# Long convolution: squares of keys on ACT, wrapped terms on POOL, key products formed one head ahead

## The chip, the cores and the metric

The kernel runs on one core of a Trainium2 chip. The metric is the device time of one execution in microseconds. Before the change three runs took 3490.82 to 3492.23 us, with a median of 3491.84 us. Five engines share a core: TensorE (PE), VectorE (DVE), ScalarE (ACT), GpSimd (POOL) and SyncE (SP), which issues the loads. Each has its own stream of instructions, and they meet only through semaphores.

## What is computed

The kernel is a decoder of two layers. The change touches one of its six mixing steps, the long convolution, which is given here in full; the others stand as names.

```python
# B, S, D = 8, 256, 512; ctx is a second input of the same shape as x; everything is fp32
def _L0_xattn_ref(k, v, q, ssm_kernel, D, head_dim):      # called with k = v = ctx, q = x, head_dim = 8
    B, HD, L = k.shape                                     # 8, 256, 512
    H = HD // head_dim                                     # 32 heads of 8 rows
    k_, v_, q_ = (t.reshape(B, H, head_dim, L) for t in (k, v, q))
    kv = jnp.einsum('bhil,bhjl->bijhl', k_, v_)            # product of row i and row j, element by element
    y = irfft(rfft(kv, 2 * L) * rfft(ssm_kernel, 2 * L))[..., :L]   # causal convolution along L with head h's filter
    out = y + kv * D[None, None, None, :, None]
    out = jnp.einsum('bijhl,bhil->bjhl', out, q_)          # times row i of x, summed over i
    return jnp.transpose(out, (0, 2, 1, 3)).reshape(B, H * head_dim, L)

x = _layernorm(x + attention(x))
x = _layernorm(x + _L0_xattn_ref(ctx, ctx, x, ssm_kernel, D, 8))   # the stage that the change touches
x = _layernorm(x + quantized_linear(x))
x = _layernorm(x + gated_delta_rule(x))
x = _layernorm(x + decayed_sum(x, ctx, ctx))
x = _layernorm(x + quantized_mlp(x))
```

Keys and values are the same tensor, so the product of rows i and j serves both (i, j) and (j, i), and of 64 pairs 36 differ.

## The kernel before, in words

The stages run one after the other, each in a block of its own, with a barrier at its end. X holds the activations, token by token. `conv_stage` (lines 621 to 816) works as follows.

**Layout.** The 512 positions of a row lie on 128 partitions in KC = 4 chunks. C (`conv_ahead_C`) holds the keys, loaded during the stage before, and xT the activations, which PE turns (line 728) and ACT copies (lines 765, 766). Both keep 12 elements for the 8 rows of a head, of which the last 4 repeat the first 4, so that "row i + d, modulo 8" is a contiguous read. A pair of rows is told by its distance d: for d = 0 to 3 there are 8 pairs, for d = 4 there are 4, so a head has 8 x 36 = 288 pairs (`PAIRS`, for 8 sequences), of which the first 256 are those of d = 0 to 3. The pairs of d = 0 are the squares of the keys.

**One head**, in a loop over 16 pairs of heads with two sets of buffers (`par`):
- POOL forms the key products `kv`, one large operation (256 elements a partition, line 700) and one small (32 elements, line 703) for each chunk. It first waits until PE is done with the head two back, whose buffer it takes.
- PE multiplies `kv` with the filter as a Toeplitz matrix `T` (line 745): 1, 2, 3 and 4 products for the output chunks 0 to 3, each into a bank of its own, 10 products or 20 matmul instructions. `T` is loaded by SP two heads ahead (line 678).
- ACT copies bank 0 to `ys` (line 773), because POOL can't be given the bank itself. POOL multiplies `ys` with rows of xT (lines 713, 715, 717) and writes the terms of chunk 0 into `pr`. DVE does the same for chunks 1 to 3 straight from the banks (lines 795, 798, 801).
- `pr` has 11 rows of 8 terms for each chunk and sequence: pair (i, i+d) adds a term to row i and one to row i+d, and where i+d exceeds 7 the latter stands in rows 8 to 10, columns 5 to 7. These are the wrapped terms, which belong to rows 0 to 2.
- DVE sums the 8 terms of rows 0 to 7 into zT (line 806), then the 3 wrapped terms of rows 8 to 10 into `wrap` (line 808), and adds `wrap` to the first three rows of zT (line 812).

After the last head PE turns zT back (line 754), and DVE adds it to X (line 816).

**What sets the order around the change.** Each engine works in the order of its program. POOL's order is: key products of head h, then its terms of head h, then the next head. POOL may write its terms once DVE has summed and wrapped the head two back (`red` at 2 of 3). DVE's order is: nine products, line 806, line 808, line 812, next head. The counters `kv`, `mm`, `yc`, `pp`, `pr` and `red` count key products, banks finished by PE, copies of ACT, terms of POOL, terms of DVE and DVE's sums. A wait reads `at(k, n)`: k steps within unit n, where head h is unit h + 2.

Of the kernel before, what the change touches and what calls it, by code (L numbers as in the profile page):

```python
# [9 lines left out]
ALU = mybir.AluOpType  # L10
ACT = mybir.ActivationFunctionType
# [609 lines left out]
def conv_stage(nc, X, consts, ahead, kpad, dskip, kp_dram):  # L621
    with ExitStack() as ctx:
# [20 lines left out]
        g = {n: counter(n, c) for n, c in dict(kv=8, mm=4, yc=1, pp=3, pr=9, red=3).items()}  # L643
# [39 lines left out]
        def _(pool):  # L683
# [10 lines left out]
            with nc.Fori(0, CH // 2, engines=(ENG.Pool,)) as hp:  # L694
                for par in range(2):

                    pool.wait_ge(g["mm"].sem, g["mm"].at(4, hp * 2 + par))
                    for kc in range(KC):
                        h = hp * 2 + par
                        gp.tensor_tensor(kv[:, par, kc, 0:B * 32].rearrange("p (b d i) -> p b d i", b=B, d=4),  # L700
                                         rows(C, kc, h, 0, (0, 4), (1, 8)), rows(C, kc, h, 0, (1, 4), (1, 8)),
                                         ALU.mult).then_inc(g["kv"].sem, 1)
                        gp.tensor_tensor(kv[:, par, kc, B * 32:PAIRS].rearrange("p (b i) -> p b i", b=B),  # L703
                                         rows(C, kc, h, 0, (1, 4)), rows(C, kc, h, 4, (1, 4)),
                                         ALU.mult).then_inc(g["kv"].sem, 1)

# [3 lines left out]
                    pool.wait_ge(g["red"].sem, g["red"].at(2, n0))  # L710
# [7 lines left out]
                                     rows(xT, 0, h, 4, (4, 2), (1, 4)), ALU.mult).then_inc(g["pp"].sem, 1)  # L718

        @block.tensor  # L720
        def _(pe):
# [10 lines left out]
            with nc.Fori(0, CH // 2, engines=(ENG.PE,)) as hp:  # L732
                for par in range(2):
                    n0, n1 = hp * 2 + par, hp * 2 + par + 2
                    pe.wait_ge(tl[par].sem, tl[par].at(1, hp))
                    for lo in range(KC):
                        pe.wait_ge(g["kv"].sem, g["kv"].at(2 * lo + 2, n1))
                        bk = bank[4 * par + lo]

                        if lo == 0:  # L740
                            pe.wait_ge(g["yc"].sem, g["yc"].at(1, n0))
                        else:
                            pe.wait_ge(g["pr"].sem, g["pr"].at(3 * lo, n0))
                        for mb in range(lo + 1):
                            last = te.matmul(bk[:, 0:PAIRS], T[:, par, (lo - mb) * P:(lo - mb + 1) * P],  # L745
                                             kv[:, par, mb, :], start=(mb == 0), stop=(mb == lo))
                        last.then_inc(g["mm"].sem, 1)

            pe.wait_ge(g["red"].sem, g["red"].at(3, CH + 1))
# [9 lines left out]
        def _(act):  # L759
# [7 lines left out]
            act.sem_inc(g["yc"].sem, 2 * g["yc"].per)  # L767
            with nc.Fori(0, CH // 2, engines=(ENG.Activation,)) as hp:
                for par in range(2):
                    n0, n1 = hp * 2 + par, hp * 2 + par + 2  # L770
                    act.wait_ge(g["mm"].sem, g["mm"].at(1, n1))
# [5 lines left out]
        def _(dve):  # L777
# [4 lines left out]
            dve.wait_ge(zero.sem, zero.at(1))  # L782
            zv = zT[:, :, :].rearrange("p k (b s) -> p (k b) s", b=B)
            with nc.Fori(0, CH // 2, engines=(ENG.DVE,)) as hp:
                for par in range(2):
# [3 lines left out]
                    dve.wait_ge(g["red"].sem, g["red"].at(2, n0))  # L789
                    for lo in range(1, KC):  # L790
# [16 lines left out]
                    dve.wait_ge(g["red"].sem, g["red"].at(3, n1 - 1))  # L807
                    ve.tensor_reduce(wrap[:, :, :], pr[:, par, :, 8:11, 5:8], AX.X, ALU.add)\
                        .then_inc(g["red"].sem, 1)
                    dve.wait_ge(g["red"].sem, g["red"].at(2, n1))  # L810
                    z3 = zv[:, :, bass.ds(h * HR, 3)]
                    ve.tensor_tensor(z3, z3, wrap[:, :, :], ALU.add).then_inc(g["red"].sem, 1)
            dve.wait_ge(g["red"].sem, g["red"].at(3, CH + 1))
# [1891 lines left out]
```

## Time and profile before

| | us |
|---|---|
| median of three runs | 3491.84 |
| lowest and highest run | 3490.82, 3492.23 |
| the profiled execution | 3496.09 |
| its span, first to last instruction | 3494.4 |
| in it, the loop over heads, first key product to last addition of wrapped terms | 446.1 to 658.0 |
| busy in the span: PE, DVE | 3089.3, 2625.7 |
| busy in the span: ACT, POOL | 2128.0, 1517.3 |

Busy times are sums over a whole span of many stages. What a change in one stage is worth must be read from that stage: the table by stretch, the groups of instructions with the idle time before them, the waits, and the timeline. Idle time "before" a group is put down to what ended it. A matmul's end is modelled, so a busy PE isn't PE at its best. Starts of instructions on one engine can lie closer than their durations, since one begins while the last drains.

### The profile page before, as it was taken

The numbers are of one execution on the slowest core, as the hardware profiler recorded it, in microseconds if no ns is written. First come the engines' busy times: TensorE is split into PE (matmuls) and PEld (weight loads), VectorE is DVE, ScalarE is ACT, GpSimd is POOL, SyncE is SP. The second block draws the span as 40 slices with busy tenths as digits, with TensorE's granted clock in tenths as the row PEclk, the third lists the DMA queues.
The fourth block names the chain that finished last, engine by engine and source line by source line (L and its number), as shares of the span: only waits on it lengthen the run. The fifth ranks groups of instructions, "written<-read, shape, count | busy, mean of one in ns | idle before, by whom it ended". The sixth has DMA issues, their size and how long they took to land. (4 is left out here: it accounts for less than half of the span.)

```text
span 3494.4 us, 77166 instructions
## 1 busy us (share of the span) xinstructions
PE 3089.3 (88%) x29261; PEld 2182.4 (62%) x29280; DVE 2625.7 (75%) x4740; ACT 2128.0 (61%) x5446; POOL 1517.3 (43%) x1853
## 2 busy tenths in 40 slices
PE   6999788447999999999999999999999999993186
PEld 4666565324777777777777777777777777772143
DVE  3444479884878878788787887878878788776887
ACT  4444310135777777777777777777777777764454
POOL 1111177214646555465554655546555455540000
PEclk9999999777999999999999999999999999996599
DMA  4000011001010001101000101101111010101201
GB/s 193 13 13 1 3 42 42 27 21 46 19 39 32 26 32 28 35 32 26 32 33 30 32 26 32 38 25 32 26 32 43 20 34 23 32 8 49 96 1 49
DMA packets 42858, 118.97 MB, mean 34 GB/s; under 512 B 6032, under 2 KB 10256, under 8 KB 39184
## 3 DMA queue, kind: packets, MB, share of 16 engines
q1 hardware_dynamic: 42512, 114.25, 10.3%
q8 instruction: 230, 3.77, 0.4%
q14 instruction: 116, 0.95, 0.1%
HBM read 109.70 MB, written 4.54 MB: 33 GB/s over the span
## 5 line engine op out<-in xcount | busy, mean ns | idle before, releaser
L2030 DVE TENSOR_TENSOR delta_Pb<-delta_bank,delta_lev 128x512 f16<-128x512 f32 x448 | 310.9, 694 | 201.0 <-PE delta_bank L2360 201.0
L1600 POOL TENSOR_SCALAR_AFFINE_SELECT delta_LA<-delta_LA 128x512 f32<-128x512 f32 x128 | 81.6, 637 | 798.6 <-DVE delta_LA L2059 763.6
L2022 DVE SCALAR_TENSOR_TENSOR delta_F<-delta_bank,delta_cw,delta_F 128x510 f32<-128x510 f32 (+1 forms) x512 | 381.5, 745 | 57.8 <-ACT delta_far L1838 40.3
L2334 PE MATMUL delta_bank<-delta_xh,delta_qkvh 128*128 128x512 f16 x1024 | 390.4, 381 | 4.6 <-DVE delta_qkvl L1995 3.1
L2334 PE MATMUL delta_bank<-delta_xl,delta_qkvh 128*128 128x512 f16 x1024 | 390.4, 381 | 0.0
L2334 PE MATMUL delta_bank<-delta_xh,delta_qkvl 128*128 128x512 f16 x1024 | 390.3, 381 | 0.0
L1620 POOL TENSOR_TENSOR delta_F<-delta_F,delta_far 128x506 f32<-128x506 f32 x256 | 278.8, 1089 | 192.7 <-DVE delta_F L2022 192.7
L1832 ACT ACTIVATE delta_F<-delta_bank,delta_cw 128x512 f32<-128x512 f32 x256 | 175.2, 684 | 264.4 <-PE delta_bank L2334 264.2
L2047 DVE CAST delta_XT<-delta_bank 128x512 f16<-128x512 f32 x384 | 263.3, 686 | 85.2 <-PE delta_bank L2379 85.0
L1797 ACT ACTIVATE delta_Xi<-delta_bank 128x512 f16<-128x512 f32 x320 | 190.1, 594 | 155.1 <-PE delta_bank L2375 155.0
L2319 PE MATMUL delta_bank<-delta_zh,delta_xh 128*128 128x256 f16 x1024 | 280.2, 274 | 0.6 <-ACT delta_gz L1860 0.6
L2319 PE MATMUL delta_bank<-delta_zh,delta_xl 128*128 128x256 f16 x1024 | 280.0, 273 | 0.0
L2319 PE MATMUL delta_bank<-delta_zl,delta_xh 128*128 128x256 f16 x1024 | 279.8, 273 | 0.0
L296 POOL TENSOR_TENSOR attn_dg<-ident,attn_ri 128x1024 f32<-128x1024 f32 x32 | 60.7, 1897 | 340.5 <-DVE attn_ri L519 340.5
L2328 PE MATMUL delta_bank<-delta_oh,delta_ch 128*128 128x512 f16 x512 | 195.4, 382 | 6.2 <-DVE X L2161 4.7
L745 PE MATMUL conv_bank<-conv_kv,conv_T 128*128 128x288 f32 x640 | 172.7, 420 | 30.8 <-POOL conv_kv L703 28.8
L2328 PE MATMUL delta_bank<-delta_oh,delta_cl 128*128 128x512 f16 x512 | 194.8, 380 | 0.0
L2328 PE MATMUL delta_bank<-delta_ol,delta_ch 128*128 128x512 f16 x512 | 194.7, 380 | 0.0
L2059 DVE SCALAR_TENSOR_TENSOR delta_LA<-delta_bank,delta_rk,delta_EL 128x512 f32<-128x512 f32 x256 | 179.3, 743 | 6.2 <-ACT delta_EL L1746 4.8
L2161 DVE SCALAR_TENSOR_TENSOR X<-delta_bank,X 128x512 f32<-128x512 f32 x256 | 173.6, 683 | 13.2 <-PE delta_bank L2328 8.7
L1847 ACT ACTIVATE delta_F<-delta_F 128x512 f32<-128x512 f32 x256 | 163.1, 637 | 31.5 <-POOL delta_F L1620 28.8
L1612 POOL TENSOR_TENSOR delta_og<-delta_og,delta_gz 128x512 f32<-128x512 f32 x128 | 163.3, 1277 | 33.8 <-ACT delta_og L1780 33.8
(364 smaller groups left out, 9310.8 us busy)
## 6 DMA issues: line engine op xcount, KB each, us to landing
delta_Gb<-g_rows SPq DMA_DIRECT2D x64, 512.0 KB, 5.3
delta_st_qkv<-in_Wqkv SPq DMA_DIRECT2D x17, 1024.0 KB, 8.5
conv_T<-filters SPq DMA_DIRECT2D x32, 256.0 KB, 3.0
delta_st_zo<-in_Wz SPq DMA_DIRECT2D x16, 512.0 KB, 9.0
delta_st_zo<-in_Wout SPq DMA_DIRECT2D x16, 512.0 KB, 6.6
ffn_ahead_W<-in_W SPq DMA_DIRECT2D x2, 4096.0 KB, 17.1
conv_ahead_C<-in_ctx_rev SPq DMA_DIRECT2D x1, 6144.0 KB, 27.2
attn_xt<-in_xT SPq DMA_DIRECT2D x8, 512.0 KB, 5.0
```

Source lines behind the costliest of these rows:

```text
L745: last = te.matmul(bk[:, 0:PAIRS], T[:, par, (lo - mb) * P:(lo - mb + 1) * P], kv[:, par, mb, :], start=(mb == 0), stop=(mb == lo))
L1620: gp.tensor_tensor(dst[:, :, 3:256], dst[:, :, 3:256], src[:, :, 0:253], ALU.add)\
L1797: sc.activation(left(Xi[:, :, :], lvl), comp(bank[5], lvl), ACT.Copy).then_inc(g["xc"].sem, 1)
L1832: sc.activation(F[:, i, :], bank[AT[job] % 2][:, :], ACT.Copy, scale=cw_tap(i, 3))\
L2022: ve.scalar_tensor_tensor(dst, src, cw_tap(i, 3 - lag), dst, ALU.mult, ALU.add)\
L2030: ve.tensor_tensor(left(Pb[:, lvl, :, :], lvl), comp(bank[5], lvl), bc(lev[:, lvl, :].rearrange("p (n s) -> p n s", s=1 << lvl), 1, 8), AL ...
L2047: ve.tensor_copy(right(XT[:, it.u(off) % 2, :, :], lvl), comp(bank[7], lvl))\
L2059: ve.scalar_tensor_tensor(LA[:, it.u(1) % 2, q, :, 0:256], bank[(6, 2)[b_]][:, :].rearrange("p (a i) -> p a i", a=2), rk2[:, 2 * b_:2 * b_ ...
L2161: ve.scalar_tensor_tensor(X[:, tile, :], bank[AT[f"w{t}"] % 2][:, :], CS, X[:, tile, :], ALU.mult, ALU.add).then_inc(g["wadd"].sem, 1)
L2319: ins = te.matmul(bk[:, sub * 256:(sub + 1) * 256], xx[:, kc, tok:tok + P], ww[:, kc, :], start=(r == 0), stop=(r == 11))
L2328: ins = te.matmul(bk[:, :], cc[:, blk, :], ww[:, v_, :], start=(m == 0), stop=(m == 5))
L2334: ins = te.matmul(bk[:, :], ww[:, QKV[job], kc, :], xx[:, kc, tok:tok + 512], start=(m == 0), stop=(m == 11))
```

## The change

**The key products.** POOL's large key product of each chunk leaves out d = 0 and has 192 elements a partition. The squares (d = 0, all four chunks, 1024 elements a partition) are one activation of ACT per head, under a new counter `sq`, placed ahead of ACT's copy of the same head and behind a wait for PE's products of the head two back. PE waits for `sq` as well before its first product of a head.

**The wrapped terms.** Lines 808 and 812 leave DVE. POOL adds column 5 and column 6 of rows 8 to 10 into `wrap`, adds column 7 to it, and adds `wrap` to zT: three additions of 96 elements a partition, counted by the new `wr`. Before the first it waits for DVE's nine products and its own three of that head, before the second for the first, and before the third for the second and for DVE's large sum.

**The order on POOL.** Key products of head 0 come ahead of the loop. Then for each head h: the terms of head h, the key products of head h + 1, the wrapped terms of head h. The last pair of heads stands behind the loop, without key products for a head that doesn't exist. The waits for a free `pr` now name `red` (at 1 of 1) and `wr` (at 2 of 3), and PE's transposes wait for the last `wr`.

```diff
--- before.py
+++ after.py
@@ -640,7 +640,7 @@
         tl = [counter(f"tload{i}", 1, 16) for i in range(2)]
         zero = counter("zero")
         kadd, xt, xc = counter("kadd"), counter("xt"), counter("xc")
-        g = {n: counter(n, c) for n, c in dict(kv=8, mm=4, yc=1, pp=3, pr=9, red=3).items()}
+        g = {n: counter(n, c) for n, c in dict(kv=8, sq=1, mm=4, yc=1, pp=3, pr=9, red=1, wr=3).items()}
         zt, za = counter("zt"), counter("za")
         block = ctx.enter_context(nc.Block())
 
@@ -691,23 +691,38 @@
             pool.wait_ge(ahead.loaded["C"].sem, ahead.loaded["C"].at(1))
             pool.wait_ge(zero.sem, zero.at(1))
             pool.wait_ge(xc.sem, xc.at(KC * 4))
-            with nc.Fori(0, CH // 2, engines=(ENG.Pool,)) as hp:
+            pool.sem_inc(g["wr"].sem, 2 * g["wr"].per)
+
+            def kv_products(n, par):
+                pool.wait_ge(g["mm"].sem, g["mm"].at(4, n))
+                for kc in range(KC):
+                    gp.tensor_tensor(
+                        kv[:, par, kc, 0:B * 32].rearrange("p (b d i) -> p b d i", b=B, d=4)[:, :, 1:4, :],
+                        rows(C, kc, n, 0, (0, 3), (1, 8)), rows(C, kc, n, 1, (1, 3), (1, 8)), ALU.mult)\
+                        .then_inc(g["kv"].sem, 1)
+                    gp.tensor_tensor(kv[:, par, kc, B * 32:PAIRS].rearrange("p (b i) -> p b i", b=B),
+                                     rows(C, kc, n, 0, (1, 4)), rows(C, kc, n, 4, (1, 4)),
+                                     ALU.mult).then_inc(g["kv"].sem, 1)
+
+            def wrapped(n, par):
+                pool.wait_ge(g["pr"].sem, g["pr"].at(9, n + 2))
+                pool.wait_ge(g["pp"].sem, g["pp"].at(3, n + 2))
+                last3 = [pr[:, par, :, 8:11, i:i + 1].rearrange("p a b c -> p a (b c)") for i in (5, 6, 7)]
+                gp.tensor_tensor(wrap[:, :, :], last3[0], last3[1], ALU.add).then_inc(g["wr"].sem, 1)
+                pool.wait_ge(g["wr"].sem, g["wr"].at(1, n + 2))
+                gp.tensor_tensor(wrap[:, :, :], wrap[:, :, :], last3[2], ALU.add).then_inc(g["wr"].sem, 1)
+                pool.wait_ge(g["wr"].sem, g["wr"].at(2, n + 2))
+                pool.wait_ge(g["red"].sem, g["red"].at(1, n + 2))
+                z3 = zT[:, :, :].rearrange("p k (b s) -> p (k b) s", b=B)[:, :, bass.ds(n * HR, 3)]
+                gp.tensor_tensor(z3, z3, wrap[:, :, :], ALU.add).then_inc(g["wr"].sem, 1)
+
+            def pair(hp, more):
                 for par in range(2):
-
-                    pool.wait_ge(g["mm"].sem, g["mm"].at(4, hp * 2 + par))
-                    for kc in range(KC):
-                        h = hp * 2 + par
-                        gp.tensor_tensor(kv[:, par, kc, 0:B * 32].rearrange("p (b d i) -> p b d i", b=B, d=4),
-                                         rows(C, kc, h, 0, (0, 4), (1, 8)), rows(C, kc, h, 0, (1, 4), (1, 8)),
-                                         ALU.mult).then_inc(g["kv"].sem, 1)
-                        gp.tensor_tensor(kv[:, par, kc, B * 32:PAIRS].rearrange("p (b i) -> p b i", b=B),
-                                         rows(C, kc, h, 0, (1, 4)), rows(C, kc, h, 4, (1, 4)),
-                                         ALU.mult).then_inc(g["kv"].sem, 1)
-
                     n0, n1 = hp * 2 + par, hp * 2 + par + 2
                     h = hp * 2 + par
                     pool.wait_ge(g["yc"].sem, g["yc"].at(1, n1))
-                    pool.wait_ge(g["red"].sem, g["red"].at(2, n0))
+                    pool.wait_ge(g["red"].sem, g["red"].at(1, n0))
+                    pool.wait_ge(g["wr"].sem, g["wr"].at(2, n0))
                     y = ys[:, par, 0:B * 32].rearrange("p (b d i) -> p b d i", b=B, d=4)
                     y4 = ys[:, par, B * 32:PAIRS].rearrange("p (b i) -> p b i", b=B)
                     gp.tensor_tensor(terms(par, 0, 0, (1, 4), (8, 8)), y, rows(xT, 0, h, 0, (1, 4), (1, 8)),
@@ -716,6 +731,14 @@
                         .then_inc(g["pp"].sem, 1)
                     gp.tensor_tensor(terms(par, 0, 4, (32, 2), (8, 4)), bc(y4, 2, 2),
                                      rows(xT, 0, h, 4, (4, 2), (1, 4)), ALU.mult).then_inc(g["pp"].sem, 1)
+                    if par == 0 or more:
+                        kv_products(h + 1, 1 - par)
+                    wrapped(h, par)
+
+            kv_products(0, 0)
+            with nc.Fori(0, CH // 2 - 1, engines=(ENG.Pool,)) as hp:
+                pair(hp, True)
+            pair(CH // 2 - 1, False)
 
         @block.tensor
         def _(pe):
@@ -735,6 +758,8 @@
                     pe.wait_ge(tl[par].sem, tl[par].at(1, hp))
                     for lo in range(KC):
                         pe.wait_ge(g["kv"].sem, g["kv"].at(2 * lo + 2, n1))
+                        if lo == 0:
+                            pe.wait_ge(g["sq"].sem, g["sq"].at(1, n1))
                         bk = bank[4 * par + lo]
 
                         if lo == 0:
@@ -746,7 +771,7 @@
                                              kv[:, par, mb, :], start=(mb == 0), stop=(mb == lo))
                         last.then_inc(g["mm"].sem, 1)
 
-            pe.wait_ge(g["red"].sem, g["red"].at(3, CH + 1))
+            pe.wait_ge(g["wr"].sem, g["wr"].at(3, CH + 1))
             for t in range(NT):
                 if t >= 4:
                     pe.wait_ge(za.sem, za.at(t - 3))
@@ -765,9 +790,16 @@
                 nc.scalar.activation(dst[:, :, 0:HR], src, ACT.Copy)
                 nc.scalar.activation(dst[:, :, HR:HW], src[:, :, 0:HW - HR], ACT.Copy).then_inc(xc.sem, 1)
             act.sem_inc(g["yc"].sem, 2 * g["yc"].per)
+            act.sem_inc(g["sq"].sem, 2 * g["sq"].per)
+            act.wait_ge(ahead.loaded["C"].sem, ahead.loaded["C"].at(1))
             with nc.Fori(0, CH // 2, engines=(ENG.Activation,)) as hp:
                 for par in range(2):
                     n0, n1 = hp * 2 + par, hp * 2 + par + 2
+                    act.wait_ge(g["mm"].sem, g["mm"].at(4, n0))
+                    squared = kv[:, par, :, 0:B * 32].rearrange("p k (b d i) -> p k b d i", b=B, d=4)[:, :, :, 0, :]
+                    keys = C[:, :, :].rearrange("p k (b h r) -> p k b h r", b=B, h=CH)
+                    keys = keys[:, :, :, bass.ds(hp * 2 + par, 1), 0:HR].rearrange("p k b h r -> p k (b h) r")
+                    nc.scalar.activation(squared, keys, ACT.Square).then_inc(g["sq"].sem, 1)
                     act.wait_ge(g["mm"].sem, g["mm"].at(1, n1))
                     act.wait_ge(g["pp"].sem, g["pp"].at(3, n0))
                     nc.scalar.activation(ys[:, par, :], bank[4 * par][:, 0:PAIRS], ACT.Copy)\
@@ -780,13 +812,15 @@
             for n in ("pr", "red"):
                 dve.sem_inc(g[n].sem, 2 * g[n].per)
             dve.wait_ge(zero.sem, zero.at(1))
+            dve.wait_ge(g["wr"].sem, g["wr"].at(2, 1))
             zv = zT[:, :, :].rearrange("p k (b s) -> p (k b) s", b=B)
             with nc.Fori(0, CH // 2, engines=(ENG.DVE,)) as hp:
                 for par in range(2):
                     n0, n1 = hp * 2 + par, hp * 2 + par + 2
                     h = hp * 2 + par
 
-                    dve.wait_ge(g["red"].sem, g["red"].at(2, n0))
+                    dve.wait_ge(g["red"].sem, g["red"].at(1, n0))
+                    dve.wait_ge(g["wr"].sem, g["wr"].at(2, n0))
                     for lo in range(1, KC):
                         dve.wait_ge(g["mm"].sem, g["mm"].at(lo + 1, n1))
                         y = bank[4 * par + lo][:, 0:B * 32].rearrange("p (b d i) -> p b d i", b=B, d=4)
@@ -804,13 +838,6 @@
                     dve.wait_ge(g["pp"].sem, g["pp"].at(3, n1))
                     z = zv[:, :, bass.ds(h * HR, HR)]
                     ve.tensor_reduce(z, pr[:, par, :, 0:8, :], AX.X, ALU.add).then_inc(g["red"].sem, 1)
-                    dve.wait_ge(g["red"].sem, g["red"].at(3, n1 - 1))
-                    ve.tensor_reduce(wrap[:, :, :], pr[:, par, :, 8:11, 5:8], AX.X, ALU.add)\
-                        .then_inc(g["red"].sem, 1)
-                    dve.wait_ge(g["red"].sem, g["red"].at(2, n1))
-                    z3 = zv[:, :, bass.ds(h * HR, 3)]
-                    ve.tensor_tensor(z3, z3, wrap[:, :, :], ALU.add).then_inc(g["red"].sem, 1)
-            dve.wait_ge(g["red"].sem, g["red"].at(3, CH + 1))
             for t in range(NT):
                 dve.wait_ge(zt.sem, zt.at(t + 1))
                 ve.tensor_tensor(X[:, t, :], X[:, t, :], bank[t % 4][:, :], ALU.add).then_inc(za.sem, 1)
```

## Rows read from the trace of the kernel before

**Rows 1.** The page's first lines: span, and busy time of each engine.
```profile
span 3494.4 us, 77166 instructions
PE 3089.3 (88%) x29261; PEld 2182.4 (62%) x29280; DVE 2625.7 (75%) x4740; ACT 2128.0 (61%) x5446; POOL 1517.3 (43%) x1853
```

**Rows 2.** Table by stretch, within the loop: length, busy time by engine, granted clock.
```profile
466.00:530.00 64.00, 55.47 (x211) 38.26 (x210) 58.42 (x120) 4.11 (x10) 46.76 (x111) 1.00 0.15 45
```

**Rows 3.** Instructions of tile wrap: ns min/median/max, first and last start.
```profile
L812 DVE TENSOR_TENSOR conv_zT<-conv_zT,conv_wrap x32: 257/258/314, 459.3 to 657.7; 128x96 f32 x32
```

**Rows 4.** Waits from 446 to 658 us: total, times, longest.
```profile
POOL conv_pr L713 <- DVE conv_wrap L808: 48.6, 28, 2.0
...
DVE conv_pr L795 <- DVE conv_zT L812: 6.8, 14, 0.5
```

**Rows 5.** Timeline of the steady loop: start, duration, engine, line, idle before.
```profile
536.63 0.63 DVE L795 TENSOR_TENSOR conv_pr<-conv_bank,conv_xT 128x256 f32<-128x256 f32 x1
...
542.02 0.44 DVE L808 TENSOR_REDUCE conv_wrap<-conv_pr 128x96 f32<-128x288 f32 x1
542.50 0.26 DVE L812 TENSOR_TENSOR conv_zT<-conv_zT,conv_wrap 128x96 f32 x1
542.63 0.72 POOL L713 TENSOR_TENSOR conv_pr<-conv_ys,conv_xT 128x256 f32<-128x256 f32 x1 [1.55 <-DVE conv_wrap L808]
543.24 0.63 DVE L795 TENSOR_TENSOR conv_pr<-conv_bank,conv_xT 128x256 f32<-128x256 f32 x1 [0.48 <-DVE conv_zT L812]
...
544.13 0.61 POOL L700 TENSOR_TENSOR conv_kv<-conv_ahead_C 128x256 f32 x1
...
544.70 0.25 POOL L703 TENSOR_TENSOR conv_kv<-conv_ahead_C 128x32 f32 x1
...
545.08 5.41 PE L745 MATMUL conv_bank<-conv_kv,conv_T 128*128 128x288 f32 x20 [0.79 <-POOL conv_kv L703]
545.11 0.62 DVE L795 TENSOR_TENSOR conv_pr<-conv_bank,conv_xT 128x256 f32<-128x256 f32 x1
...
545.95 0.41 ACT L773 ACTIVATE conv_ys<-conv_bank 128x288 f32<-128x288 f32 x1 [5.86 <-PE conv_bank L745]
...
546.44 2.29 DVE L806 TENSOR_REDUCE conv_zT<-conv_pr 128x2048 f32 x1 [0.25 <-DVE conv_pr L801]
...
549.45 0.62 DVE L795 TENSOR_TENSOR conv_pr<-conv_bank,conv_xT 128x256 f32<-128x256 f32 x1
```

**Rows 6.** Groups of POOL, 446 to 658 us: busy, mean ns, idle before.
```profile
L700 POOL TENSOR_TENSOR conv_kv<-conv_ahead_C 128x256 f32 x128 | 78.6, 614 | 7.1 <-ACT conv_xT L766 7.1
...
L703 POOL TENSOR_TENSOR conv_kv<-conv_ahead_C 128x32 f32 x128 | 32.5, 254 | 0.0
...
L713 POOL TENSOR_TENSOR conv_pr<-conv_ys,conv_xT 128x256 f32<-128x256 f32 x32 | 23.1, 721 | 51.4 <-DVE conv_wrap L808 48.6 <-ACT conv_ys L773 2.5 <-issue 0.4
L715 POOL TENSOR_TENSOR conv_pr<-conv_ys,conv_xT 128x192 f32<-128x192 f32 x32 | 19.2, 600 | 0.0
...
L717 POOL TENSOR_TENSOR conv_pr<-conv_ys,conv_xT 128x64 f32<-128x64 f32 x32 | 10.0, 314 | 0.0
```

**Rows 7.** POOL's waits over the whole span, the one for itself.
```profile
POOL delta_Lt L1604 <- POOL delta_LA L1600: 21.4, 128, 0.2
```

**Rows 8.** Timeline of the loop's start, where PE runs ahead.
```profile
456.64 2.29 DVE L806 TENSOR_REDUCE conv_zT<-conv_pr 128x2048 f32 x1 [0.25 <-DVE conv_pr L801]
...
460.61 0.41 ACT L773 ACTIVATE conv_ys<-conv_bank 128x288 f32<-128x288 f32 x1 [4.43 <-PE conv_bank L745]
...
465.47 0.41 ACT L773 ACTIVATE conv_ys<-conv_bank 128x288 f32<-128x288 f32 x1 [4.44 <-PE conv_bank L745]
```

**Rows 9.** Groups of ACT over the whole span.
```profile
L765 ACT ACTIVATE conv_xT<-conv_bank 128x512 f32<-128x512 f32 x16 | 11.0, 705 | 2.3 <-PE conv_bank L728 2.3
...
L993 ACT ACTIVATE decay_ahead_C<-decay_ahead_C 128x2048 f32<-128x2048 f32 x4 | 7.3, 1898 | 0.7 <-PEq L53 0.7
```

## The prediction

> **What bounds the kernel now.** The page comes first. DVE is busy for 75% of the span and PE for 88%, but these are averages over stages with different limits [rows 1], and the change touches one stage, the long convolution. So the second view is the table by stretch. Between 466 and 530 us DVE works 58.42 of 64.00 us, PE 55.47, POOL 46.76 and ACT 4.11, at a granted clock of 1.00, the upper level of 2.4 GHz [rows 2]. DVE is closest to full. The tile row of the wrapped sums gives the pace: the addition of line 812 starts first at 459.3 and last at 657.7 us, 31 heads apart, 6.40 us a head [rows 3].
>
> Third, the waits. DVE hardly waits: 6.8 us in 14 places before line 795, each behind its own line 812. POOL waits 48.6 us in 28 places for line 808 [rows 4]. The timeline shows both. Line 795 starts at 536.63, 543.24 and 549.45 us, so heads take 6.61 and 6.21 us by turns. From the first product to the large reduction takes 3.20 us (543.24 to 546.44). The long reduction of line 806 takes 2.29, and its follower, line 808, can start some 2.20 after it. Lines 808 and 812 start 0.48 apart (542.02, 542.50). The next product starts 0.74 after 812 (543.24) in one head; the other head is 0.40 shorter, which leaves 0.34. The 0.4 are the turn of the loop: the row at 543.24 has 0.48 of idle time behind an instruction that it doesn't wait for, and this occurs in every second head [rows 5]. DVE's own order is the bound.
>
> **What DVE sheds.** Lines 808 and 812 go, 0.48 and 0.34 us from start to start, and the turn of the loop gets a cover: DVE's last instruction of a head is now the 2.29 us reduction, and the waits behind it are long fulfilled. DVE alone would need 3.20 + 2.20 = 5.40 us a head [rows 5]. The two added waits on `wr` cost DVE nothing in themselves: they ask for a sum two heads back.
>
> **What POOL sheds.** The large key product shrinks from 256 to 192 elements. Rows for 256 and 32 elements, 614 and 254 ns, give 1.6 ns an element, so 192 cost 0.51 us instead of 0.61 [rows 6]. Between ends, line 715 (192 elements, 0.60) would save almost nothing and a cost in proportion (0.46) a little more; I take 0.51, because the operands are those of line 700. One chunk's pair of products, 0.57 + 0.21 from start to start, becomes 0.68; four are 2.71 us.
>
> **What POOL takes on.** Three additions of 96 elements a head, whose mean price I call p. No row shows POOL at this shape. Below lies line 703 (32 elements, 0.254), above it line 715 (192, 0.600), and next to it line 717 (64, 0.314) [rows 6]. Between 717 and 715, 96 elements come to 0.39 us, which I take. The second and third addition each wait for the one before: where POOL waits for itself before line 1604, the gap is 21.4 / 128 = 0.17 us [rows 7]. The products of line 713 to 717 take 1.50 from the first start to line 700 (542.63 to 544.13). The turn of POOL's loop now stands behind a wait, as DVE's does now, and costs 0.4 every second head, where before it was covered by lines 715 and 717 [rows 5]. POOL's own round is then 1.50 + 2.71 + (p + 0.17) + (p + 0.17) + (p - 0.04, the usual overlap) + 0.20 = 4.71 + 3p, or 5.88 us a head at p = 0.39.
>
> **The new loop through four engines.** Before, POOL's products of a head waited for DVE's sums of two heads back. Now POOL can't start them until it has added the wrapped terms of the head just before, which waits for DVE's large reduction. Queued behind that wait are the products of line 713 and the keys of the following head, and PE waits for these. Let Z(h) be the start of POOL's last addition for head h. Then:
> - addition 0.35, products of h+1 1.50, to the first key product of h+2: 1.85;
> - first keys of h+2: 0.47 + 0.25, then 0.06 to 0.13 until PE starts (544.95 to 545.08) [rows 5]. In all 2.63;
> - PE's 20 matmuls: ACT's copies at 460.61 and 465.47 show 4.86 us a head when PE runs without a pause [rows 8]. The copy starts 0.87 after PE (545.08 to 545.95) [rows 5], of which two matmuls are 0.49: some 0.4 from the last issue to a reader. PE's last bank can be read at 7.88;
> - the last three products of DVE and its wait, 545.11 to 546.44 [rows 5], 1.31 to 1.33: 9.19; the reduction 2.29: 11.48; and 0.17 until POOL adds (542.46 to 542.63): 11.65 us for two heads.
> The loop starting from an odd head also holds POOL's turn of 0.4: 12.05 us, or **6.03 us a head**. This is longer than POOL's 5.88 and DVE's 5.40, so it is what I expect to bind, until p exceeds 0.44. PE alone needs 4.86.
>
> **The squares.** ACT gets one operation of 128x1024 a head. The nearest row is a square of 2048 elements, 1898 ns [rows 9]: about 1.0 us, up to 1.4 if its short runs are as costly as those of line 765, 0.705 for 512 [rows 9]. ACT waits 5.86 of every 6.3 us for PE now [rows 5]. A square is issued right behind the copy of the preceding head, at about Z + 4, and is needed at Z + 8.6. It costs nothing while PE is the later, and would cost only past 4 us. Its wait for PE's products of two heads back is fulfilled some 2 us earlier. The first square stands beside POOL's first key product. The loads of line 678 stay under PE's order.
>
> **The sum.** Head 0 is unchanged up to its reduction, which starts at 456.64 [rows 8] and ends at 458.93. POOL adds at 459.1, multiplies head 1 from 459.45 and forms keys of head 2 from 460.95; its additions for head 1 end with Z(1) = 460.95 + 2.71 + 1.12 = 464.78. From there 15 double steps of 12.05 lead to Z(31) = 645.5. Line 812 stood at 657.7 [rows 3]: 12.2 us less. The transposes behind it are unchanged. The profiled span of 3494.4 us [rows 1] would become 3482.2; its execution took 3496.09 with 1.7 around the span, and the median of the runs is 4.25 lower, 3491.84. So the forecast is 3491.84 - 12.2 = **3479.6 us**. A difference below 0.2%, 7 us, is no more than a measurement of this kernel can tell from no change.
>
> **Rivals.**
> - The turn of POOL's loop is covered. POOL's row after the turn now (544.13 and its like) shows no gap, but there two long products stand before it. Then the loop is 11.65 for two heads, 5.83 a head; Z(31) = 464.4 + 15 x 11.65 = 639.1, so 18.6 us less: 3473.2. Chance 0.18.
> - POOL's additions are dearer by their reads of every eighth element. Line 713, which writes at this step, takes 0.72 against 0.61 for line 700 at 256 elements [rows 6], or 0.42 ns an element for one wide operand. If a read costs twice that, 0.08 us for 96 elements, the first addition (two wide reads) costs 0.55, the second 0.47, the third 0.39: p = 0.47 and a round of 6.12, 30 x (6.40 - 6.12) + 0.8 = 9.2 us less, 3482.6. Chance 0.17. The Trainium skill (GPSIMD Engine Reference, Performance pitfalls for Q7 kernels) says that reads at a step over 8 bytes cost about 50% more per element; no row of the kernel before shows POOL reading at such a step.
> - POOL's additions cost 0.50, midway between my price and line 715's [rows 6], as short runs may make them. The round is 6.21: 30 x 0.19 + 0.8 = 6.5 us less, 3485.3. Against it: the same products cost POOL little more than DVE (0.72 for line 713, 0.62 for line 795) [rows 5, 6], and DVE adds 96 elements in 0.258 [rows 3]. Chance 0.12. The Trainium skill (GPSIMD Engine Reference, Key points) has DVE about twice as fast in elementwise work, which speaks against this move: twice 0.258 would be an estimate of 0.52, and 3487 by it; the rows of this stage show a ratio of 1.2.
> - Slower: POOL takes DVE's place as the bound and is worse. It decides from p = 0.565, where 4.71 + 3p passes 6.40. At line 713's 0.72 [rows 6] the round is 6.87, 30 x 0.47 - 0.8 = 13.3 us more: 3505. For it: three operations in a row, each waiting for the last; against it: that price is for 256 elements. Chance 0.09.
> - The change frees DVE entirely, because PE's start isn't as tied as I have it: 5.40 a head, 30 us less, 3461. Chance 0.04.
>
> **Chances and range.** The forecast has 0.40. Faster by over 0.2% (under 3484.9) holds it, the covered turn, the wide reads, the freed DVE and a little of the additions at 0.50: 0.81. Within 0.2% holds most of the latter and half of the slower case: 0.14. Slower: 0.05. The range goes from 3470, just under the covered turn with cheaper additions, to 3489, the additions at 0.50 and a little above; it leaves out the freed DVE, the slower case and a rest.
>
> **What the profile will show.** Right: no line 808 or 812 on DVE, about 6.0 us between large reductions with heads in unequal pairs, DVE idle some 0.6 us a head before its last product for PE (bank of chunk 3), POOL waiting a little for the reduction before its third addition, and PE starting each head just behind the first keys. Wrong: POOL without any wait (its additions over 0.44 us), DVE without any idle time, ACT's square later than the first keys, or a granted clock under 1.00 in the stage, because every term of PE is taken at 2.4 GHz.

## The result, and the profile after

The changed kernel takes 3501.53 us in the median of ten runs (3499.57 to 3503.09), the kernel before 3490.82 us in ten (3490.25 to 3493.2). The ratio is 1.0029, with a 95% interval of 1.0019 to 1.0039: slower by 10.7 us, where 12.2 us less had been forecast. The two profiled executions, with spans of 3499.0 and 3494.4 us, stand closer together than that, because the profiled one of before was 5 us above its own median; so what follows reads the stage, not the span. The stage's own start differs as well: PE's first transposition of X begins at 431.91 us before and at 430.00 after.

| | before | after |
|---|---|---|
| median us | 3490.82 | 3501.53 |
| last addition of wrapped terms, first and last start | 459.3, 657.7 | 457.0, 667.6 |
| us a head between them | 6.40 | 6.79 |
| granted clock, in a stretch of the loop | 1.00 | 0.87 |

First the instructions of the tile `wrap`, as in [rows 3]; all three additions are on POOL now:

```profile
L711 POOL TENSOR_TENSOR conv_wrap<-conv_pr x32: 352/360/373, 454.4 to 665.0; 128x96 f32<-128x96 f32 x32
L713 POOL TENSOR_TENSOR conv_wrap<-conv_wrap,conv_pr x32: 431/432/437, 454.9 to 665.4; 128x96 f32<-128x96 f32 x32
L717 POOL TENSOR_TENSOR conv_zT<-conv_zT,conv_wrap x32: 373/376/382, 457.0 to 667.6; 128x96 f32 x30, 128x96 f32<-128x96 f32 x2
```

They cost 0.36, 0.43 and 0.38 us. The stage takes 12.2 us more from the first last-addition to the 32nd (210.6 against 198.4), about the whole loss; counted from PE's first transposition, its last addition comes 11.8 us later. The groups between 446 and 680 us, as in [rows 6] (busy, mean ns, idle before):

```profile
L770 PE MATMUL conv_bank<-conv_kv,conv_T 128*128 128x288 f32 x639 | 188.4, 462 | 29.1 <-POOL conv_kv L703 29.1
...
L840 DVE TENSOR_REDUCE conv_zT<-conv_pr 128x2048 f32 x32 | 73.1, 2286 | 8.0 <-DVE conv_pr L835 8.0
L699 POOL TENSOR_TENSOR conv_kv<-conv_ahead_C 128x192 f32 x120 | 60.8, 506 | 0.0
L829 DVE TENSOR_TENSOR conv_pr<-conv_bank,conv_xT 128x256 f32<-128x256 f32 x96 | 59.8, 623 | 61.4 <-PE conv_bank L770 59.2 <-POOL conv_wrap L713 1.8
...
L802 ACT ACTIVATE conv_kv<-conv_ahead_C 128x256 f32 x31 | 12.8, 412 | 0.2
```

DVE now waits 59.2 us for PE. PE is busy for 188.4 us with the same products, and a matmul takes 462 ns in the mean. The timeline of PE alone shows when (start, duration, count, idle before):

```profile
528.23 11.74 PE L770 MATMUL conv_bank<-conv_kv,conv_T 128*128 128x288 f32 x40 [1.94 <-POOL conv_kv L703]
541.91 11.74 PE L770 MATMUL conv_bank<-conv_kv,conv_T 128*128 128x288 f32 x40 [1.94 <-POOL conv_kv L703]
555.60 11.75 PE L770 MATMUL conv_bank<-conv_kv,conv_T 128*128 128x288 f32 x40 [1.94 <-POOL conv_kv L703]
```

Two heads, 40 matmuls, come in one piece of 11.74 us, then PE pauses for 1.94, and this repeats every 13.68 us, fifteen times from 459.81 on. The table by stretch, as in [rows 2], over most of the loop and then in single microseconds of one pair (length, PE, its weight loads, DVE, ACT, POOL, granted clock):

```profile
530.00:594.00 64.00, 56.23 (x194) 40.87 (x193) 49.21 (x92) 6.99 (x18) 49.04 (x130) 0.87 0.14 37
541.90:542.90 1.00, 0.99 (x4) 0.67 (x5) 0.92 (x1) 0.12 (x1) 1.00 (x4) 1.00 0.33 107
542.90:543.90 1.00, 1.00 (x4) 0.79 (x3) 1.00 (x1) 0.59 (x2) 1.00 (x4) 0.58 0.00 0
543.90:544.90 1.00, 1.00 (x3) 0.66 (x2) 0.85 (x3) 0.00 (x0) 0.72 (x3) 0.50 0.00 0
544.90:545.90 1.00, 1.00 (x3) 0.67 (x2) 0.59 (x3) 0.00 (x0) 0.77 (x2) 0.50 0.00 0
545.90:546.90 1.00, 1.00 (x4) 0.73 (x3) 0.00 (x0) 0.00 (x0) 1.00 (x4) 0.71 0.00 0
546.90:547.90 1.00, 1.00 (x5) 0.76 (x4) 0.89 (x3) 0.00 (x0) 1.00 (x3) 1.00 0.00 0
547.90:548.90 1.00, 1.00 (x6) 0.78 (x5) 0.21 (x2) 0.00 (x0) 1.00 (x5) 1.00 0.00 0
```

About one microsecond after PE resumes, its clock falls from 2.4 to 1.2 GHz, for some 3.4 us. The full slices of a microsecond at the low clock hold 3 matmuls, those that overlap an edge counted in, and the slices at the full clock that follow 5 or 6. DVE waits for them:

```profile
545.22 0.28 DVE L835 TENSOR_TENSOR conv_pr<-conv_bank,conv_xT 128x64 f32<-128x64 f32 x1
...
547.01 0.63 DVE L829 TENSOR_TENSOR conv_pr<-conv_bank,conv_xT 128x256 f32<-128x256 f32 x1 [1.52 <-PE conv_bank L770]
...
548.95 0.62 DVE L829 TENSOR_TENSOR conv_pr<-conv_bank,conv_xT 128x256 f32<-128x256 f32 x1 [0.84 <-PE conv_bank L770]
...
550.29 2.29 DVE L840 TENSOR_REDUCE conv_zT<-conv_pr 128x2048 f32 x1 [0.25 <-DVE conv_pr L835]
...
552.83 0.38 POOL L717 TENSOR_TENSOR conv_zT<-conv_zT,conv_wrap 128x96 f32 x1 [1.74 <-DVE conv_zT L840]
```

and POOL waits for DVE before its third addition (552.83). Only then come its terms and the keys that PE needs next, and PE resumes at 555.60. In the kernel before the clock stayed at 1.00 from 454 us to the end of the loop, with pauses of PE up to 1.13 us:

```profile
538.80 5.49 PE L745 MATMUL conv_bank<-conv_kv,conv_T 128*128 128x288 f32 x20 [1.12 <-POOL conv_kv L703]
551.62 5.49 PE L745 MATMUL conv_bank<-conv_kv,conv_T 128*128 128x288 f32 x20 [1.13 <-POOL conv_kv L703]
```

There PE led DVE by about 5 us: the head that it ends at 544.29 (538.80 and 5.49) is begun by DVE at 549.45 [rows 5].

### The profile page after: what moved, and what is told of

The parts are those of the page before. It is cut to its first block and busy times, and to the rows that moved or that the text cites. A ratio compares the mean times of both kernels' runs of the same rounds, so it can differ in the third digit from the quotient of the medians.

```text
span 3499.0 us, 77484 instructions
## 1 busy us (share of the span) xinstructions
PE 3100.5 (89%) x29261; PEld 2197.7 (63%) x29280; DVE 2605.8 (74%) x4676; ACT 2137.6 (61%) x5478; POOL 1538.6 (44%) x1949
## 5 line engine op out<-in xcount | busy, mean ns | idle before, releaser
L770 PE MATMUL conv_bank<-conv_kv,conv_T 128*128 128x288 f32 x640 | 189.1, 463 | 32.7 <-POOL conv_kv L703 32.7
L770 PEld LDWEIGHTS conv_bank<-conv_kv,conv_T 128*128 128x128 f32 x640 | 136.5, 217 | 85.1 <-issue 43.9
```

## The theories

**A.** The loop through four engines exists as forecast, but its new pause in PE lowers PE's clock, and since the loop goes through PE, the 1.8 us lost at the low clock lengthen every pair of heads. **B.** The loop is long by itself, and the low clock only fills time in which PE would wait. **C.** POOL's added work is too dear.

## Experiments

Each ratio below is to the kernel before, measured beside that run. Its median was 3490.82 us beside the changed kernel, 3492.86 or 3492.74 beside the first eight runs and 3494.42 beside the last two (one idle product, and merged products on the changed kernel). So a difference of medians between runs of different groups is uncertain by up to 4 us.

### Idle work for PE

```diff
             pe.sem_inc(g["mm"].sem, 2 * g["mm"].per)
+            pe.wait_ge(xc.sem, xc.at(KC * 4))
...
+                    pe.wait_ge(g["yc"].sem, g["yc"].at(1, n0))
+                    for _ in range(2):
+                        te.matmul(bank[4 * par][:, PAIRS:512], ident[:, :], xT[:, 0, 0:512 - PAIRS], start=True,
+                                  stop=True)
```

> The changed kernel, with two products of 224 columns (four matmul instructions, about 0.75 us) put on PE at the start of each head, before its wait for keys; their results go to unused columns and are read by nobody. Theory A (the pause of 1.94 us in PE lets the granted clock fall to 1.2 GHz for some 3.5 us of each pair of heads, and this costs 1.8 us a pair): the clock stays at 1.00 in the loop, a pair takes 12.1 instead of 13.7 us, about 24 us less than the changed kernel, so 3477 to 3481, faster than the kernel before. Theory B (the loop through POOL, PE and DVE is long by itself and the low clock only fills time that PE would have waited anyway): PE's extra work hides in its pauses, the clock may rise, the time stays within 3 us of 3501.5.

Measured: 3481.54 us (3477.93 to 3482.51), 0.9965 of the kernel before (0.9952 to 0.9977), 20 us less than the changed kernel, with more work. Stretch and PE's timeline:

```profile
530.00:594.00 64.00, 60.40 (x252) 46.42 (x251) 56.47 (x104) 8.53 (x22) 55.68 (x148) 1.00 0.16 43
```
```profile
540.25 0.92 PE L761 MATMUL conv_bank<-conv_xT,ident 128*128 128x224 f32 x4
541.88 5.20 PE L775 MATMUL conv_bank<-conv_kv,conv_T 128*128 128x288 f32 x20 [0.72 <-POOL conv_kv L703]
546.91 0.92 PE L761 MATMUL conv_bank<-conv_xT,ident 128*128 128x224 f32 x4
547.67 5.01 PE L775 MATMUL conv_bank<-conv_kv,conv_T 128*128 128x288 f32 x20
```

The clock is at 1.00, a head takes 6.11 us (DVE's large reductions start from 457.0 to 646.5, 31 heads). B falls: it forecast no gain from the clock. The pace is close to the forecast of 6.03 us, in part by luck, as the end shows.

With half the idle work:

> The run with idle work on PE, with one product of 224 columns (0.38 us) at the start of each head instead of two. Theory A: PE's pause of 1.94 us becomes about 1.5; the run with two products had 0.7 at most and kept its clock, the kernel before kept it with 1.1. If pauses of 1.5 don't lower it, 3478 to 3483 as with two; if they do, 3499 to 3504. Theory B (the loop is long by itself): within 3 us of 3501.5 in either case, and it has already lost by the run with two products.

Measured: 3481.56 us, 0.9955 (0.9939 to 0.9972), four executions. Clock 1.00, 6.11 us a head, and from 501 us on PE's pauses alternate between almost nothing and 1.11 us. The pause wasn't 1.5, as expected, since with the full clock the pauses are shorter; so the run says nothing of 1.5 us. Two runs further down come nearer: pauses of 1.40 to 1.43 us (squares alone) and one of 1.64 us (merged products) weren't followed by a fall.

### A pause in the kernel before

```diff
-                        pe.wait_ge(g["kv"].sem, g["kv"].at(2 * lo + 2, n1))
+                        pe.wait_ge(g["kv"].sem, g["kv"].at(8 if par == 0 else 2 * lo + 2, n1))
```

> The kernel before, where PE waits in every even head for all eight key products instead of the first two, so that its pause before that head grows by 2.3 us, to 3.1 to 3.5. Theory A: the granted clock falls after that pause in every pair, as in the changed kernel, to a mean of 0.85 to 0.9 in the loop; since PE has about 5 us of lead over DVE there, the time stays within 3 us of 3491. Theory B has no forecast for the clock here. If the clock stays at 1.00, a pause of PE is not what lowers it and theory A falls.

Measured: 3494.6 us, 1.0005 (0.9996 to 1.0015). PE's timeline:

```profile
483.43 9.96 PE L745 MATMUL conv_bank<-conv_kv,conv_T 128*128 128x288 f32 x40 [1.21 <-POOL conv_kv L703]
496.04 11.65 PE L745 MATMUL conv_bank<-conv_kv,conv_T 128*128 128x288 f32 x40 [2.65 <-POOL conv_kv L703]
508.90 9.96 PE L745 MATMUL conv_bank<-conv_kv,conv_T 128*128 128x288 f32 x40 [1.21 <-POOL conv_kv L703]
521.71 9.96 PE L745 MATMUL conv_bank<-conv_kv,conv_T 128*128 128x288 f32 x40 [2.85 <-POOL conv_kv L703]
534.54 9.96 PE L745 MATMUL conv_bank<-conv_kv,conv_T 128*128 128x288 f32 x40 [2.87 <-POOL conv_kv L703]
547.35 11.59 PE L745 MATMUL conv_bank<-conv_kv,conv_T 128*128 128x288 f32 x40 [2.85 <-POOL conv_kv L703]
```

Two heads take 9.96 us at the full clock, and 11.53 to 11.65 where it fell: 1.6 to 1.7 us is the price of a fall. It fell after four of the eight pauses of 2.65 to 2.88 us, and after none of 1.2. So a pause can lower the clock, but not each does, and the mean clock of 0.97 (530 to 594 us) was higher than I expected; the longest pauses came out at 2.88 us, not at 3.1 to 3.5. The time didn't move: with PE ahead of DVE the price is hidden.

### The wrapped terms one head later on POOL

```diff
+                pool.wait_ge(g["wr"].sem, g["wr"].at(3, n + 1))
                 gp.tensor_tensor(wrap[:, :, :], last3[0], last3[1], ALU.add).then_inc(g["wr"].sem, 1)
...
                     if par == 0 or more:
                         kv_products(h + 1, 1 - par)
-                    wrapped(h, par)
+                    if par == 1 or wrap0:
+                        wrapped(h - 1, 1 - par)
```

The added wait keeps `wrap` until the third addition of the head before has read it. The first pair of heads stands ahead of the loop, and the wrapped terms of the last head behind everything.

> The changed kernel, with the wrapped terms of head h - 1 instead of head h behind the key products of head h + 1 on POOL, so that POOL never waits for a sum that DVE is still making. The additions are as many. Theory A and my loop: the chain through four engines is cut, POOL's own round of 5.73 us a head binds (1.48 + 2.70 + 0.44 + 0.63 + 0.34 + 0.14), PE pauses 0.9 us at each head and keeps its clock, 3468 to 3473. Theory C (the move to POOL is wrong in itself, because POOL's additions are too dear): POOL is no faster than now, and the time stays over 3490.

Measured: 3470.23 us, 0.9935 (0.9918 to 0.9952). Every operation of the changed kernel is there, at the same price, and C falls. Apart from ACT, which waits for PE, nobody waits for another engine at length between 470 and 640 us:

```profile
PE conv_bank L774 <- POOL conv_kv L703: 16.9, 27, 0.8
...
POOL conv_zT L718 <- POOL conv_wrap L714: 6.7, 27, 0.3
DVE conv_pr L833 <- PE conv_bank L774: 5.5, 17, 0.4
```

The longest pause of PE is 0.8 us, the clock 1.00, and a head takes 5.72 us (reductions from 456.1 to 633.5), POOL's own round, for which 5.73 had been expected.

### The third addition back on DVE

`z3 += wrap` follows line 840 on DVE again, under `red`; POOL keeps the other two. Before the first of them it now waits until DVE has added the sums of the preceding head.

> The changed kernel with the third addition (wrapped sums to zT) given back to DVE; POOL makes the two others and no longer waits for DVE's large reduction. Theory A with my loop: the loop through four engines is cut, DVE's order binds at 3.20 + 2.20 + 0.34, a self-wait of 0.05 to 0.25 and half a loop turn of 0.4, together 6.0 to 6.2 us a head; PE pauses about 1.2 us at each head and keeps its clock; 3479 to 3485. Theory C (POOL's additions are too dear): POOL still makes two of three and the time stays over 3495.

Measured: 3484.2 us, 0.9977 (0.9967 to 0.9986); clock 1.00, PE's pauses 0.95 to 1.08 us, 6.21 us a head. POOL still makes most of the added work, and the loss is gone with the one handover from DVE to POOL. DVE is slower than the sum had it, by its addition:

```profile
L841 DVE TENSOR_TENSOR conv_zT<-conv_zT,conv_wrap x32: 257/496/637, 455.8 to 648.2; 128x96 f32 x32
```

The median is 0.50 us, against 0.26 in [rows 3]; more on this at the end.

### The squares

Alone on the kernel before, with nothing else of the change:

> The kernel before with the squares alone moved to ACT, and PE's wait for them. All theories: DVE's order of 6.40 us a head is untouched, so no change, within 3 us of 3491; PE starts each head about 0.1 us sooner after POOL's first key. If it is slower by more, ACT's writes to the key tile delay PE or POOL, and the squares have a share in the loss.

Measured: 3492.88 us, 0.9999 (0.999 to 1.0009), no change; PE pauses 0.97 to 1.00 and 1.40 to 1.43 us by turns in the steady loop, at a clock of 1.00. And the changed kernel without them:

> The changed kernel with the squares given back to POOL (256 elements a chunk, nothing on ACT, no wait of PE for them). Theory A: the loop through four engines is 0.1 us longer to the first keys, POOL's own round 0.4 us longer (6.13 us a head), PE still pauses near 2 us once in a pair, the clock still falls there: 3499 to 3506. If the pauses come out more equal (under 1.3 us each) the clock holds and the time is 3482 to 3488. Against both: if the squares or PE's added wait for them were a cause of the loss, this would be faster than 3495 with the clock as low as before.

Measured: 3501.07 us, 1.0015 (1.0001 to 1.0029). The profiled execution has PE in pairs of heads of 11.95 to 11.70 us with pauses of 1.96, clock 0.87 to 0.89, as the changed kernel. The eight executions of this one program spread from 3486.18 to 3504.04 us: six, with a mean granted clock of 0.947 over the whole kernel, took 3500.7 to 3504.0; the two with 0.952 and 0.954 took 3489.35 and 3486.18. So it seems that this program can fall into the rhythm with the low clock or miss it; only one of the eight has a trace. The squares have no share in the loss.

Where POOL binds, they are worth something:

> The run with deferred wrapped terms, and the squares given back to POOL. POOL binds there, and four products of 256 instead of 192 elements cost it 4 x 0.10: 6.13 us a head, 31 x 0.41 = 13 us more than with the squares on ACT, 3480 to 3485. If the squares are worth nothing once POOL doesn't wait for DVE, it stays within 3 us of 3470.

Measured: 3482.08 us, 0.997 (0.9958 to 0.9981), 11.9 us more than with the squares on ACT; 6.12 us a head.

### Less work for POOL

```diff
+                gp.tensor_tensor(kv[:, par, :, B * 32:PAIRS].rearrange("p k (b i) -> p k b i", b=B), near, far,
+                                 ALU.mult).then_inc(g["kv"].sem, 1)
                 for kc in range(KC):
...
-                    gp.tensor_tensor(kv[:, par, kc, B * 32:PAIRS].rearrange("p (b i) -> p b i", b=B),
-                                     rows(C, kc, n, 0, (1, 4)), rows(C, kc, n, 4, (1, 4)),
-                                     ALU.mult).then_inc(g["kv"].sem, 1)
```

`near` and `far` are the same rows as before, over all four chunks. On the changed kernel:

> The changed kernel with POOL's four small key products made one of 128 elements, nothing else: POOL's own round falls from 5.73 to about 5.3 us a head, while the loop from POOL's last addition through PE and DVE back to POOL becomes about 0.1 us longer, because the first large product waits behind the merged one. Theory A: the loop and the low clock bind, so the time doesn't fall, 3498 to 3505, unless the rhythm of the pauses changes and the clock holds (3480 to 3484). Theory C (POOL's work is what is too dear): 32 x 0.45 = 14 us less than 3501.5 with the clock as low as before, 3487.

Measured: 3498.62 us (3496.49 to 3501.22), 1.001 (1.0 to 1.0019). The forecast of 3498 to 3505 held. Within this one execution PE's timeline shows both rhythms:

```profile
542.77 11.65 PE L772 MATMUL conv_bank<-conv_kv,conv_T 128*128 128x288 f32 x40 [2.15 <-POOL conv_kv L704]
556.58 11.61 PE L772 MATMUL conv_bank<-conv_kv,conv_T 128*128 128x288 f32 x40 [2.16 <-POOL conv_kv L704]
570.34 5.11 PE L772 MATMUL conv_bank<-conv_kv,conv_T 128*128 128x288 f32 x20 [2.16 <-POOL conv_kv L704]
576.02 5.09 PE L772 MATMUL conv_bank<-conv_kv,conv_T 128*128 128x288 f32 x20 [0.56 <-POOL conv_kv L704]
582.45 5.11 PE L772 MATMUL conv_bank<-conv_kv,conv_T 128*128 128x288 f32 x20 [1.35 <-POOL conv_kv L704]
588.39 5.09 PE L772 MATMUL conv_bank<-conv_kv,conv_T 128*128 128x288 f32 x20 [0.82 <-POOL conv_kv L704]
...
625.52 5.09 PE L772 MATMUL conv_bank<-conv_kv,conv_T 128*128 128x288 f32 x20 [1.64 <-POOL conv_kv L704]
630.88 5.11 PE L772 MATMUL conv_bank<-conv_kv,conv_T 128*128 128x288 f32 x20 [0.27 <-POOL conv_kv L704]
637.91 11.63 PE L772 MATMUL conv_bank<-conv_kv,conv_T 128*128 128x288 f32 x40 [1.92 <-POOL conv_kv L704]
```

Eight pairs take 13.8 us each with the low clock. At 570.34 a pause of the same 2.16 us isn't followed by a fall, the two heads split, and the next pair takes 12.11 (570.34 to 582.45), at the clock of 1.00, 1.7 us less. It doesn't last. The even heads go on every 12.11 us, the odd ones every 12.37 to 12.39 (576.02 to 588.39). The difference fits POOL's turn of 0.28 us, which only the loop from an odd head holds. So the pause before an odd head grows by 0.27 us a pair, 0.56, 0.82, up to 1.64 and 1.92, and the one before an even head shrinks to nothing. At 637.91 all of it stands in one place again, and the clock falls. The median is 3 us below the changed kernel's, and 4.2 instead of 10.7 us above that of the kernel before beside it; the pairs with the low clock take 13.8 us, for 13.68, so that the 0.45 us a head taken from POOL saves nothing by itself, against C.

On the deferred kernel, where POOL binds:

> The run with deferred wrapped terms, and POOL's four small key products (32 elements each) made one of 128 ahead of the four large ones. POOL binds in that run at 5.72 us a head; 4 x 0.21 us become about 0.37, its round 5.26, and DVE's 5.40 binds: 30 x 0.32 = 10 us less, 3458 to 3463, clock 1.00. If PE's 4.86 or a handover binds instead, the gain stays under 5 us.

Measured: 3461.88 us (3461.01 to 3466.72), 0.9916 (0.9899 to 0.9932), 31 us less than the kernel before on the same chip (3492.74) and 40 less than the changed one. The reductions start 5.40 us apart (456.4 to 623.9), DVE's own order:

```profile
530.00:594.00 64.00, 60.92 (x241) 44.33 (x240) 60.99 (x118) 9.17 (x24) 58.72 (x133) 1.00 0.18 49
```

## Why the prediction was wrong, point by point

- **The bound of before**, DVE's own order at 6.40 us: right. Freed of the two operations and with its loop turn covered, DVE needs 5.40 us, which the last run shows to the hundredth.
- **Prices on POOL**: p came to 0.39 us (0.360, 0.432, 0.376), as taken; the large key product 0.506, for 0.51. POOL's gaps behind its own additions, taken at 0.17 us each, are 0.09 before the second and 0.20 before the third. Its loop turn costs 0.28 (544.73 to 545.33 is 0.60, without the turn 0.32 to 0.34), for 0.4. The rows of the changed kernel:

```profile
543.66 0.35 POOL L711 TENSOR_TENSOR conv_wrap<-conv_pr 128x96 f32<-128x96 f32 x1
544.10 0.43 POOL L713 TENSOR_TENSOR conv_wrap<-conv_wrap,conv_pr 128x96 f32<-128x96 f32 x1
544.73 0.37 POOL L717 TENSOR_TENSOR conv_zT<-conv_zT,conv_wrap 128x96 f32 x1 [0.20 <-POOL conv_wrap L713]
545.33 0.72 POOL L728 TENSOR_TENSOR conv_pr<-conv_ys,conv_xT 128x256 f32<-128x256 f32 x1 [0.23 <-POOL conv_zT L717]
```

The rivals with dearer additions fall by this row. The Trainium skill (GPSIMD Engine Reference, Performance pitfalls for Q7 kernels) would have the wide reads cost half more per element; the trace disagrees: line 711, with two wide reads, is the cheapest of the three at 0.360. The Trainium skill (GPSIMD Engine Reference, Key points) has a factor of about two against DVE; here it is 0.376 to 0.258, 1.46.
- **The squares**: free, as said, but mis-sized. I took 1024 elements a partition, there and in the description of the change; 8 sequences, 8 rows and 4 chunks are 256, and the row says 0.412 us, not 1.0.
- **The loop through four engines**: right in its path, and it does bind. Its mean of 6.11 us a head at the full clock (idle work), for 6.03, is close in part by luck. In the run with merged products the two loops take 12.11 and 12.38 us, of which 0.19 are the merged product ahead of the first keys (1.14 us from POOL's first key product to PE, 581.31 to 582.45, for 0.95 in the changed kernel, 554.65 to 555.60). That leaves 11.92 and 12.19, where the forecast had 11.65 and 12.05. Both are longer in the step from first keys to PE (0.95, for 0.78) and in the one from DVE's sum to POOL's addition (0.25, for 0.17); the turn, too dear by 0.12, hides half of this in the longer loop.
- **The step that failed** is the term for PE: "every term of PE is taken at 2.4 GHz". It was named as a sign that would make the forecast wrong, but it had no rival, no price and no chance. I had PE's speed from rows where it ran without a pause or with pauses up to 1.13 us, while my own sum said that PE would work 2 x 4.86 of 12.05 us and stand still for 2.3. I took these to be spread over both heads and didn't ask whether they would come in one piece. In the changed kernel they do, 1.94 us at once, and 15 pauses were followed by 15 falls. The matmuls of two heads take 11.74 us instead of the 9.96 of an unbroken piece at the full clock (a pause in the kernel before), 1.78 more. The loop that binds there starts from the even head: POOL's addition at 552.83 closes it, and no turn stands behind. A pair takes 11.92 + 1.78 = 13.70 us, and 13.68 is measured, where the forecast had 12.05. Fifteen pairs are 15 x 1.63 = 24 us above the forecast; the median is 21.9 above it.
- **Why the rhythm holds itself.** The low clock delays the first head of a pair. Keys of the second are ready by then, so PE goes on without a pause, and the whole standstill collects before the next pair. The run with merged products shows the way out of it, one fall less and the pauses divide (0.56, 1.35), and the way back: the odd heads fall behind by 0.27 us a pair until one pause holds everything. Whether the changed kernel would drift like this from a divided start wasn't seen, as it never left the low clock's rhythm in its trace. Over all runs, no pause up to 1.64 us in the steady loop was followed by a fall; those of 1.92 to 1.97 us always were (15 in the changed kernel, 15 without the squares, 1 with merged products), those of 2.15 to 2.17 us nine times of ten, those of 2.65 to 2.88 us four times of eight. Why a pause is sometimes followed by a fall and sometimes not (2.16 us both ways in that run, 2.85 both ways in the kernel before with a pause) wasn't settled.
- **What was given away before the clock**: at a full clock the change gains about 11 us (3481.5, against 3492.9 for the kernel before on that chip), and with its additions one head later 23 (3470.2). The wait for the sum of the same head took away the distance between DVE and POOL, and nothing in the computation asked for that.

## What to carry to other kernels

When work moves to an engine that feeds the matmuls, follow the loop that its new wait closes, and leave a head's distance in it: the same operations one iteration later made the difference between 3501.5 and 3470.2 us. Where such a loop goes through TensorE, work out its pauses as pieces, not as a share of time, and give the lower clock a rival with a price; a pause there can cost twice, once as time and once in the matmuls behind it (1.94 and 1.78 us here). It cost nothing where TensorE had a lead of 5 us.

## What was not expected of the hardware

- Idle work made the kernel faster: 0.75 us of products that nobody reads, each head, took 20 us off, because the clock stayed at 1.00.
- One program can hold two rhythms. The kernel without squares took 3486 to 3489 us or 3501 to 3504 us, and the one with merged products changed over in the middle of its loop, and back near its end.
- DVE's addition of 96 elements, both inputs in SBUF, takes 0.26 us alone and up to 0.63 where a key product of POOL starts with it (start, duration, engine, third addition back on DVE):

```profile
530.49 0.63 DVE L841 TENSOR_TENSOR conv_zT<-conv_zT,conv_wrap 128x96 f32 x1
530.50 0.51 POOL L699 TENSOR_TENSOR conv_kv<-conv_ahead_C 128x192 f32 x1
```

The products of DVE with one input in PSUM keep their 0.62 us beside POOL's. The Trainium skill (SBUF — State Buffer, Who interferes with whom) says that a DVE instruction with two SBUF inputs contends with a GpSimd instruction that reads SBUF; the trace agrees. In the kernel before POOL waited for line 808 and started its products only 0.13 us after this addition (542.50, 542.63 in [rows 5]), and [rows 3] shows at most 0.31.
